# Transposed feed-forward sums, and the first layer norm folded into the next product's weights

## The reference, cut to what matters

```python
q, k, v = (_lin_lora(x, W_i, A_i, B_i) for i in (0, 1, 2))
x1 = x + _lin_lora((q + k + v) / 3, W_3, A_3, B_3)
h = silu(_lin_lora(x1, W_g, A_g, B_g)) * _lin_lora(x1, W_u, A_u, B_u)      # 1792 wide
x = _layernorm(x + x1 + _lin_lora(h, W_d, A_d, B_d))                       # first norm
x = _layernorm(x + x @ W_f.T + 0.25 * (x @ A_f.T) @ B_f.T)                 # second norm
x = _layernorm(x + attention(x))                                           # third norm
x = _layernorm(x + top16_of_64_experts(x))                                 # fourth norm
# _layernorm(x) = (x - mean) / sqrt(var + 1e-5), over the 512 numbers of a token
```

## Time and profile before

| what | value |
|---|---|
| median of 3 runs | 526.15 us (522.83 to 526.68) |
| the profiled execution | 525.24 us, its span 523.4 us |
| TensorE busy (PE) | 485.5 us, 93% of the span |
| VectorE busy (DVE) | 366.0 us, 70% |
| ScalarE busy (ACT) | 293.8 us, 56% |
| GpSimd busy (POOL) | 267.6 us, 51% |

### The profile page before, as it was taken

One profiled execution on the slowest core, in us unless ns is written; L12 is line 12 of the kernel. 1 busy time (PEld: TensorE's weight loads), 2 busy tenths in 40 slices (PEclk: granted clock), 3 DMA queues, 4 the chain that ended last, 5 costly groups with the idle time before them and its releaser, 6 DMA issues.

```text
span 523.4 us, 7547 instructions
## 1 busy us (share of the span) xinstructions
PE 485.5 (93%) x2272; PEld 392.1 (75%) x2272; DVE 366.0 (70%) x704; ACT 293.8 (56%) x542; POOL 267.6 (51%) x261
## 2 busy tenths in 40 slices
PE   1579889799999999999999999999998899999996
PEld 0246678588878888888888887788886688888884
DVE  5979889656558787997897973677458866366433
ACT  6979867565675666574765642158487422333021
POOL 4687745875547566674765653147479310110001
PEclk9999999999999999999999999999999999999999
DMA  8665422423223233332443300640000000000011
GB/s 195 223 233 155 139 75 83 140 62 100 77 65 114 76 114 100 102 121 87 116 122 80 101 1 13 258 162 1 1 1 1 2 0 22 21 20 21 1 41 40
DMA packets 21415, 43.01 MB, mean 82 GB/s; under 512 B 3328, under 2 KB 3456, under 8 KB 21120
## 3 DMA queue, kind: packets, MB, share of 16 engines
q1 hardware_dynamic: 21152, 42.16, 26.1%
q0 software_dynamic: 224, 0.38, 0.3%
HBM read 40.42 MB, written 2.10 MB: 81 GB/s over the span
## 4 chain that ended last, share of the span: by engine, by line
PE 71%; issue 4%; DVE 3%; ACT 3%; POOL 1%; ACTq 0%; DVEq 0%
PE bank L1058 64%; PE bank L1213 3%; PE bank L1071 2%; PE bank L1317 1%; PE bank L1196 1%; ACT prob L1014 1%; PE bank L1080 0%; DVE rmax L1539 0%; ACT pT_hi L830 0%; DVE bn L1497 0%; DVE pT_lo L1364 0%; ACT eb_hi L830 0%; DVE rows L1463 0%; DVE xb_lo L1364 0%; DVE value L1396 0%
## 5 line engine op out<-in xcount | busy, mean ns | idle before, releaser
L749 POOL TENSOR_TENSOR wf<-value,scale 128x512 f32<-128x512 f32 x50 | 64.6, 1293 | 73.7 <-DVE value L1396 68.7
L1058 PE MATMUL bank<-x_hi,gu_hi 128*128 128x512 f32 x224 | 88.7, 396 | 0.8 <-POOL gu_lo L790 0.8
L1058 PE MATMUL bank<-x_hi,gu_lo 128*128 128x512 f32 x224 | 87.3, 390 | 0.0
L1058 PE MATMUL bank<-x_lo,gu_hi 128*128 128x512 f32 x224 | 87.3, 390 | 0.0
L813 POOL TENSOR_TENSOR rstd<-veps,neg_half 128x1 f32<-128x1 f32 x32 | 17.7, 552 | 120.7 <-issue 109.5
L838 ACT ACTIVATE bank<-code 128x512 f32<-128x512 int32 x124 | 68.6, 586 | 0.0
L1374 DVE SCALAR_TENSOR_TENSOR low<-bent,bank 128x512 f32<-128x512 f32 x62 | 42.3, 683 | 26.4 <-ACT bank L838 19.4
L796 POOL TENSOR_TENSOR h_lo<-act_f,h_hi 128x512 fp32r<-128x512 f32 x28 | 36.5, 1302 | 31.7 <-ACT h_hi L830 31.7
L1058 PEld LDWEIGHTS bank<-x_hi,gu_hi 128*128 128x128 f32 x224 | 42.2, 188 | 9.0 <-issue 1.2
L1058 PEld LDWEIGHTS bank<-x_hi,gu_lo 128*128 128x128 f32 x224 | 42.0, 188 | 9.0
L1058 PEld LDWEIGHTS bank<-x_lo,gu_hi 128*128 128x128 f32 x224 | 42.2, 188 | 7.9
(11 more groups left out here) (202 smaller groups left out, 1155.4 us busy)
## 6 DMA issues: line engine op xcount, KB each, us to landing
code<-codes SPq DMA_DIRECT2D x62, 256.0 KB, 2.7
scale<-scales SPq DMA_DIRECT2D x100, 128.0 KB, 3.0
xs<-xT SPq DMA_DIRECT2D x2, 1024.0 KB, 6.4
ea_raw<-ex_A SPq DMA_DIRECT2D x1, 2048.0 KB, 10.1
eb_raw<-ex_B SPq DMA_DIRECT2D x1, 2048.0 KB, 7.6
out<-rows SPq DMA_DIRECT2D x8, 256.0 KB, 2.0
bgu_raw<-loB_gu SPq DMA_DIRECT2D x1, 896.0 KB, 4.7
wqkv_raw<-w_qkv SPq DMA_DIRECT2D x1, 768.0 KB, 4.4
```

What stands on the lines that cost most here:

```text
L749: pool.tensor_tensor(w, v, scale[:, i % RING_CODES, :], ALU.mult).then_inc(scaled_done, 1)
L1058: last = nc.tensor.matmul(ps, a, b, start=start and i == 0 and n == 0, stop=stop and i == len(terms) - 1 and n == 2)
```

## The change

The down products swap their operands: the weights are stationary and 512 tokens of `h` move, so that the result has features on the partitions, as `xs` has. `down(gi, n)` now stands for token block b = n // 4 and output slice o = n % 4. VectorE adds each bank to `xs`, in group 0 too; the transposes of `xs` and ScalarE's copies in group 0 are gone. The last group uses three banks.

The first norm is not carried out. With s the sum before it, the second layer's product on (s - mean)/std is the product of s with weights whose mean over the input features is subtracted, divided by std; the second norm removes that division, up to its epsilon, which becomes EPS * (var(s) + EPS) for that token. So `stat:0`, `norm:0` and `turn:0` go. In their place stand: `center`, eight matmuls with a constant matrix of 1/512 that give the column means of `wff`, four VectorE subtractions, and a second split of the four chunks; `xa`, for each of the eight sums of the last group a ScalarE copy (hi), a ScalarE square and a VectorE remainder (lo); `fold`, two GpSimd additions for six of the eight, which add up the four slices of s and of its square; `mean`, for each block eight fp32 matmuls with one moving column, and four small VectorE instructions that make `eps_in`. `rows` moves to where `xs` lies, `wff` to where `rows` was, the `ffn` products get other banks, and the tail's order is rewritten up to the first `s`.

```diff
+    at = order.index(("h", 2 * NF - 1))
+    order[at:at] = [("center", 0), ("center", 1)]
+    at = order.index(("hsplit", 2 * NF - 1)) + 1
+    order[at:at] = [("center", 2), ("center", 3)]
...
+        if f == NF - 1:
+            order.insert(order.index(("up", 2 * f + 1)), ("center",))
...
 TAIL_ITEMS = """
-    norm:0.0 down:6.0 stat:0.0 down:6.1 down:6.2 down:6.3 turn:0.0 stat:0.1 down:6.4 norm:0.1 stat:0.2
-    norm:0.2 down:6.5 ffn:0 stat:0.3 turn:0.1 down:6.6 norm:0.3 turn:0.2 stat:1.0 down:6.7 stat:0.4 ffn:1
-    norm:1.0 turn:0.3 ffn:2 stat:0.5 norm:0.4 stat:1.1 turn:1.0 stat:0.6 norm:0.5 turn:0.4 norm:1.1 ffn:3
-    stat:1.2 stat:1.3 turn:1.1 turn:0.5 ffn:4 stat:0.7 norm:0.6 norm:1.2 turn:0.6 stat:1.4 turn:1.2 norm:0.7
-    ffn:5 norm:1.3 stat:1.5 turn:0.7 stat:1.6 turn:1.3 ffn:6 ffn:7 norm:1.4 norm:1.5 turn:1.4 stat:1.7
-    turn:1.5 qkv:0.0 norm:1.6 qkv:0.1 turn:1.6 norm:1.7 qkv:0.2 turn:1.7 s:0.0 s:0.1 vturn:0 qkv:1.0
+    down:6.0 down:6.1 xa:0.0 down:6.2 xa:0.1 fold:0.1 down:6.3 xa:0.2 fold:0.2 down:6.4 xa:0.3 fold:0.3 down:6.5 xa:1.0
+    down:6.6 xa:1.1 fold:1.1 down:6.7 xa:1.2 xa:1.3 ffn:0 ffn:1 mean:0 fold:1.2 stat:1.0 stat:1.1 fold:1.3 norm:1.0 norm:1.1
+    ffn:2 stat:1.2 stat:1.3 norm:1.2 ffn:3 norm:1.3 ffn:4 mean:1 stat:1.4 turn:1.0 turn:1.1 norm:1.4 ffn:5 stat:1.5
+    turn:1.2 turn:1.3 norm:1.5 ffn:6 stat:1.6 ffn:7 norm:1.6 turn:1.4 stat:1.7 turn:1.5 qkv:0.0 qkv:0.1 norm:1.7 turn:1.6 qkv:0.2 turn:1.7 s:0.0 s:0.1 vturn:0 qkv:1.0
...
-        xs = at("xs", 34, [P, KT, TOK])
+        xs = at("xs", 34, [P, NB, KT, SEQ])
...
-        rows = at("rows", 98, [P, TT, H])
+        rows = at("rows", 34, [P, TT, H])
...
-        wff_hi = at("wff_hi", 34, [P, KT, H], F32R)
-        wff_lo = at("wff_lo", 42, [P, KT, H], F32R)
+        wff_hi = at("wff_hi", 98, [P, KT, H], F32R)
+        wff_lo = at("wff_lo", 106, [P, KT, H], F32R)
+        ffn_w = [at(f"ffn_w{k}", 138.5 + 2 * k, [P, H]) for k in range(KT - 1)]
+        mean_all = at("mean_all", 144.5, [P, P], F32R)
+        square = at("square", 146, [P, NB, KT, SEQ])
+        x_sum = at("x_sum", 66, [P, NB, SEQ])
+        eps_in = at("eps_in", 205, [P, TT])
+        mean_sq = at("mean_sq", 205.25, [P, TT])
+        mean_one = at("mean_one", 205.5, [P, 1])
...
-        def down_bank(gi, t):
-
-            return bank[7] if gi < len(GROUPS) - 1 else bank[7 - t % 2]
+        def down_bank(gi, n):
+
+            return bank[7] if gi < len(GROUPS) - 1 else bank[7 - n % 3]
...
+        def rows_at(i):
+
+            return (4, 5, 2, 6, 4, 5, 2, 4)[i] if i < TT else (5, 2, 4)[(i - TT) % 3]
...
-            sp.wait_ge(lora_added, len(MERGED))
+            sp.wait_ge(centerlo_done, KT)
...
+                elif kind == "center":
+                    k = item[1]
+                    pool.wait_ge(centerhi_done, k + 1)
+                    pool.tensor_tensor(wff_lo[:, k, :], raw_ffn(k), wff_hi[:, k, :].bitcast(F32), ALU.subtract)\
+                        .then_inc(centerlo_done, 1)
...
+                if item[0] == "fold":
+
+                    b, o = item[1:]
+                    n = 2 * (KT - 1) * b + 2 * (o - 1)
+                    pool.wait_ge(square_done, KT * b + o + 1)
+                    pool.wait_ge(down_added, TT * (len(GROUPS) - 1) + KT * b + o + 1)
+                    if o > 1:
+                        pool.wait_ge(folded, n)
+                    pool.tensor_tensor(x_sum[:, b, :], xs[:, b, 0, :] if o == 1 else x_sum[:, b, :], xs[:, b, o, :],
+                                       ALU.add).then_inc(folded, 1)
+                    pool.tensor_tensor(square[:, b, 0, :], square[:, b, 0, :], square[:, b, o, :], ALU.add)\
+                        .then_inc(folded, 1)
...
+                    nc.scalar.activation(mean_all[:, :], ident[:, :], ACT.Relu, bias=1.0 / H, scale=0.0)\
+                        .then_inc(mean_all_set, 1)
...
-                elif kind == "down" and not item[1]:
-                    t = item[2]
-                    act.wait_ge(down_ready, t + 1)
-                    act.wait_ge(bprep_done, 3)
-                    copy(rows[:, t, :], down_bank(0, t)[:, :], down_added)
...
+                if kind == "xa":
+                    b, o = item[1:]
+                    act.wait_ge(down_added, TT * (len(GROUPS) - 1) + KT * b + o + 1)
+                    act.wait_ge(centerlo_done, KT)
+                    act.wait_ge(unit_ready, 2 * NF)
+                    copy(xa_hi[:, o, b * SEQ:(b + 1) * SEQ], xs[:, b, o, :], xahi_done)
+                    nc.scalar.activation(square[:, b, o, :], xs[:, b, o, :], ACT.Square).then_inc(square_done, 1)
+                elif kind == "norm" and item[1:] != (3, TT - 1):
...
-            def down(gi, t):
-
-                n = gi * TT + t
+            def down(gi, n):
+
+                b, o = n // KT, n % KT
                 last_f = GROUPS[gi][-1]
-                if gi == len(GROUPS) - 1 and t == 1:
-                    pe.wait_ge(h_done, 2 * NF)
-                elif gi == len(GROUPS) - 1 and t > 1:
-                    pe.wait_ge(down_added, n - 1)
-                elif n:
-                    pe.wait_ge(down_added, n)
-                pe.wait_ge(hhi_done, 2 * last_f + 2)
-                pe.wait_ge(hlo_done, 2 * last_f + 2)
+                if gi < len(GROUPS) - 1 or n == 0:
+                    if gi or n:
+                        pe.wait_ge(down_added, gi * TT + n)
+                elif n < 3:
+                    pe.wait_ge(h_done, 2 * NF - 2 + n)
+                else:
+                    pe.wait_ge(down_added, gi * TT + n - 2)
+                pe.wait_ge(hhi_done, 2 * last_f + b + 1)
+                pe.wait_ge(hlo_done, 2 * last_f + b + 1)
                 pe.wait_ge(hi_done, split_no(("d", last_f)))
                 pe.wait_ge(lo_done, split_no(("d", last_f)))
-                tk = slice(t * P, (t + 1) * P)
-                ps = down_bank(gi, t)
-                if gi == 0:
-                    pe.wait_ge(xs_done, KT * (t // TPB + 1))
-                    for k in range(KT):
-                        nc.tensor.matmul(ps[:, k * P:(k + 1) * P], xs[:, k, tk], ident[:, :], is_transpose=True,
-                                         start=k == 0, stop=False)
-                product(ps[:, :], [(h_hi[:, f % RING_H, tk], h_lo[:, f % RING_H, tk],
-                                    wd_hi[:, f % RING_H, :], wd_lo[:, f % RING_H, :])
-                                   for f in GROUPS[gi]], start=gi > 0).then_inc(down_ready, 1)
+                tk, cut = slice(b * SEQ, (b + 1) * SEQ), slice(o * P, (o + 1) * P)
+                product(down_bank(gi, n)[:, :], [(wd_hi[:, f % RING_H, cut], wd_lo[:, f % RING_H, cut],
+                                                  h_hi[:, f % RING_H, tk], h_lo[:, f % RING_H, tk])
+                                                 for f in GROUPS[gi]]).then_inc(down_ready, 1)
+
+            def center():
+
+                pe.wait_ge(lora_added, len(MERGED))
+                pe.wait_ge(mean_all_set, 1)
+                pe.wait_ge(hi_done, len(SPLIT))
+                pe.wait_ge(lo_done, len(SPLIT))
+                for k in range(KT):
+                    nc.tensor.matmul(center_ps[:, :], mean_all[:, :], wff_hi[:, k, :], start=k == 0, stop=False)
+                    last = nc.tensor.matmul(center_ps[:, :], mean_all[:, :], wff_lo[:, k, :], start=False,
+                                            stop=k == KT - 1)
+                last.then_inc(center_ready, 1)
 
...
+                elif kind == "mean":
+
+                    b = item[1]
+                    pe.wait_ge(folded, 2 * (KT - 1) * (b + 1))
+                    pe.wait_ge(mean_one_set, 1)
+                    pe.wait_ge(centered, KT)
+                    for t in range(b * TPB, (b + 1) * TPB):
+                        cut = slice((t % TPB) * P, (t % TPB + 1) * P)
+                        nc.tensor.matmul(mean_ps[:, t:t + 1], x_sum[:, b, cut], mean_one[:, :], start=True, stop=True)
+                        last = nc.tensor.matmul(mean_ps[:, TT + t:TT + t + 1], square[:, b, 0, cut], mean_one[:, :],
+                                                start=True, stop=True)
+                    last.then_inc(mean_ready, 1)
...
-                    pe.wait_ge(turnlo_done, turn_no[("turn", 0, t)] + 1)
-                    pe.wait_ge(turnhi_done, turn_no[("turn", 0, t)] + 1)
-                    pe.wait_ge(hi_done, len(SPLIT))
-                    pe.wait_ge(lo_done, len(SPLIT))
+                    pe.wait_ge(xahi_done, KT * (t // TPB + 1))
+                    pe.wait_ge(xalo_done, KT * (t // TPB + 1))
+                    pe.wait_ge(centerhi_done, KT)
+                    pe.wait_ge(centerlo_done, KT)
...
+            def add_down(gi, n):
+                b, o = n // KT, n % KT
+                dve.wait_ge(down_ready, gi * TT + n + 1)
+                if gi:
+                    dve.wait_ge(down_added, (gi - 1) * TT + n + 1)
+                else:
+                    dve.wait_ge(xs_done, n + 1)
```

(63 more changed lines are left out.)

100 lines of the change are left out of this document (52 added, 48 removed).

## The result

The changed kernel takes 527.48 us (median of 20 runs, 525.32 to 530.20), the kernel before, on the same chip, 526.07 (20 runs, 522.83 to 527.76). The ratio is 1.0032 with a 95% interval of 1.0018 to 1.0046: slower by 0.9 to 2.4 us. That is under the 1% that I called no change, and inside the range; but the change does move the time, where the forecast of 526.1 has it stay. The sum of +0.9 behind that forecast came near because a term that was missing was half balanced by others that came out better.

A forecast was written before the change was run, and what follows sets the result against it. TensorE, busy 93% of the span, was taken as the bound. Terms -3.8 - 0.5 + 1.8 + 0.5 - 0.2 + 0.2 - 3.5 + 3.4 + 3.0 = +0.9 on 525.24 gave 526.1 us, range 521.0 to 530.4.

The forecast's parts named there:

- With a tenth for the restart this is +3.0: Feed-forward part behind the folds: TensorE waits 0.8 before ffn:4 and 2.1 at the second mean block, +3.0 us with restart.
- the fourth: Rival, last down group: GpSimd keeps the port for two additions, remainders wait up to 2.6, some 4 us lost, 530; chance 0.07.
- the prediction's own signs: Signs of a wrong forecast: remainders 0.69 throughout, weight waits in the first group, or a mean block well off 1.7 us.
- First group: First down group: transposes gone from eight products, -3.8 us on TensorE; the 0.81 weight-split wait shrinks to 0.3, -0.5.
- the second rival: First down group: decode chain ends later than TensorE arrives, so the gain is not collected; 530.4 us, chance 0.13.
- Centred weights: Before the last up product: eight 128x512 matmuls add 1.8 us; VectorE's subtractions delay down:5.7 by 0.5.
- the walk through VectorE's queue: Before down:5.7: two subtractions stand between the last h and the add of down:5.6, so down:5.7 starts 0.5 us later.
- First norm against the mean blocks: First norm's transposes removed, -3.5 us; sixteen one-column fp32 matmuls of the mean blocks added, +3.4 us.
- The upper price: Mean blocks: each one-column fp32 matmul costs 0.21 us like the router's, rather than a transpose's 0.11.
- Behind the folds: Last group to second norm: remainders and GpSimd additions take turns, making TensorE wait 0.8 and 2.1; +3.0 us with restart.
- The first rival: Last down group: folds and remainders do not hinder each other, 2.1 us less, 524.0 us; chance 0.20.
- Ramp: Start of the kernel, where decode is the path: an extra constant on ScalarE costs 0 to 0.6 us, taken as +0.2.

The follow-up runs named there:

- e_t0: e_dvefold plus four transposes of the identity ahead of each product of the first down group; one run, distance 263.20 us, 3.81 longer than e_dvefold.
- e_nofold: The changed kernel with each fold addition cut to one column and the mean taken over one slice of four; ratio to before 0.997.
- b_mean: The kernel before plus eight one-column fp32 matmuls on constants after ffn:1 and eight after ffn:4, without a wait; ratio to before 1.0073.
- e_fill: The changed kernel plus six wide matmuls, result unused, where TensorE waits for the folds before the second mean block; 525.85 us, ratio to before 1.0007.
- e_dvefold: The changed kernel with the second block's six fold additions on VectorE, behind the last remainder, instead of GpSimd; ratio to before 0.997.
- e_late: The changed kernel with the second mean block, and the fifth token tile's statistics and normalisation, moved behind ffn:5; ratio to before 1.0019.
- the three with both ingredients: The kernel before plus one-column matmuls and a wait after ffn:4: on constants (one run), again (ratio 1.0142), and with run data as stationary operand (1.0145).

## Why the prediction was right or wrong

The step that failed is "With a tenth for the restart this is +3.0": behind the wait at the second mean block TensorE was to go on after 0.1 us at the pace of before. The prediction had that wait and the one-column matmuls behind it, and no term for TensorE's clock: the turns and ffn:5 were taken at the durations of before. The granted clock fell to 0.50 there, and the fall cost 3.10, more than the net of all other terms. None of the four rivals had it either; the second put its loss in the first group, where there was a gain, and the fourth has remainders that wait up to 2.6, where the longest takes 1781 ns in all. One of the prediction's own signs came true by it: a mean block of 2.41 instead of 1.7.

A second step failed beside it. The sum was added to one execution, 525.24, which lies 0.9 below the median of its kernel; so the 526.1 says no change where the sum says +0.9. On the median of 526.15 it gives 527.05.

By its own steps, in the distance:

- **First group**: predicted -3.8 - 0.5, measured -4.9. To the `lb_gu` matmuls behind the first product of the second group it is 159.22 - 106.33 = 52.89 before and 155.11 - 107.11 = 48.00 after. The transposes are 3.81 of it (e_t0). The weight split was not 0.3 late; the second rival (the decode chain eats the gain) falls with it.
- **Centred weights**: 320.16 - 318.35 = 1.81, as predicted. Down:5.7 waits 1.29 where it waited 0.79, the +0.5 of the walk through VectorE's queue; the next product waits 0.78, as in the pattern of before.
- **First norm against the mean blocks**: -3.5 + 3.4, and -0.2 for the small idle pieces of the last group, make -0.3. In e_nofold, without the waits behind the folds, the distance is -2.77; less -4.89 + 1.81 + 0.5 that leaves -0.19. The upper price, the router's 0.21 of the earlier trace rows, was the right end: eight take 1.68 in b_mean, not the 0.9 of transposes.
- **Behind the folds**: predicted +3.0 as waits of 0.8 and 2.1. The trace has a pause of 0.29 before ffn:4 and 1.46; with the slower restarts they cost 261.66 - 259.37 = 2.29 (e_fill against e_nofold). Place and taking turns were right, the size 0.7 too high, of which 0.4 to 0.5 is in the sum itself: from 354.5 its durations give 356.2 and 360.9, not 356.6 and 361.4. The cause was right in part: the first power did not wait for the tenth addition but for VectorE's two slowed steps. The first rival (no contention) is refuted by the remainders of 1177 ns.
- **Ramp**: the +0.2 can't be seen. The units start at 105.30 to 109.36 in these profiles, whichever kernel.

The sum in the distance: -4.89 + 1.81 + 0.5 - 0.19 + 2.29 + 3.10 = +2.62. That it meets the +2.62 of the trace is no test: -0.19 is what was left over, and 2.29 and 3.10 are differences of the same table. Without the clock it is -0.48, 1.4 better than the sum's +0.9: the clock hid that these terms were too dark, and that the time came within 1.4 of the forecast is in part luck.

In all 20 runs of the changed kernel the mean granted clock is 0.994 or less; in 20 of the 32 runs of before beside e_fill it is 0.997 or more. That fits a fall in nearly every run, but not always of the same length: +2.62 lies a little above the interval of the times (0.9 to 2.4).

## What to carry to other kernels

Where an edit puts a wait next to matmuls of few columns, ask for the granted clock behind it: here, behind 1.5 us of waiting, 3 us more were lost, most of it by matmuls that the edit never touched. Filling the wait with useless wide matmuls recovered the clock; taking the folds off the slow engine recovered the wait as well. Where VectorE and GpSimd exclude each other, price the small instructions too: two of 0.16 and 0.17 ended here only with the addition beside them. And compare kernels by a distance in their traces that leaves out a stretch which varies by itself.

## What the runs showed of the hardware

The clock falls in the ramp too, in six of the 13 profiles (e_fill, e_dvefold, e_late and the three with both ingredients). Windows of the kernel before, and of e_dvefold, over the same stretch:

```profile
98.00:106.00 8.00, 6.28 (x28) 4.92 (x29) 4.88 (x9) 4.43 (x8) 5.15 (x4) 1.00 0.51 173
```

```profile
98.00:106.00 8.00, 7.06 (x20) 5.71 (x21) 3.37 (x6) 3.82 (x8) 3.82 (x3) 0.57 0.57 178
```

The third group of `lb_gu` matmuls then starts at 108.68 instead of 106.33; in the six profiles it starts at 107.72 or later, in the other seven at 107.11 or earlier. In the trace of before such a stretch was at 1.00, so one profile didn't show that the clock can fall there. A fold of two SBUF operands takes 1.26 to 1.29 us on GpSimd alone, and 0.69 on VectorE (e_dvefold), which had the room; beside a remainder it takes 1.53 to 1.85 on GpSimd (the first seven of the changed kernel).
